# A layer on one core: the expert stage with the second bias added by VectorE, rows gathered six tiles ahead and weights loaded one transfer at a time

## The chip, the core and the metric

The kernel runs on one core of one Trainium2 chip. The metric is the device time of one execution in microseconds (us). Four kinds of engine work side by side and wait for each other through semaphores: TensorE (PE, with its weight loads PEld), VectorE (DVE), ScalarE (ACT) and GpSimd (POOL). SyncE (SP) here only issues transfers and waits. Transfers (DMA) move data between the core's memory (128 partitions) and the device's memory; those issued by GpSimd can gather or scatter rows by a list of indices.

## The reference, cut to what matters

The layer takes 6250 rows of 256 numbers and a graph of 100,000 edges. It normalizes the rows, adds a graph network and an attention with statistics per head, and ends in a mixture of 16 experts. Only this last part is touched:

```python
xn2 = layernorm(x2)                            # 6250 x 256
logits = xn2 @ gate_w + gate_b                 # 16 experts
vals, idx = top_k(logits, 2); w = softmax(vals)
h = relu(xn2 @ w1[e] + b1[e])                  # 512 hidden, e = each chosen expert
expert_out = h @ w2[e] + b2[e]
y = xn2 + sum_k w[k] * expert_out[idx[k]]
out = x2 + layernorm(y) * gamma + beta
```

Since the two weights of a row sum to 1, xn2 can be added once to y, or to each of its two expert rows before they are mixed.

## The kernel before

The rows are held in 49 tiles of 128. Each row goes to two experts, so there are 98 tiles' worth of expert rows; padded per expert they fill at most 114 tiles (XT), which the kernel always works through. Run on these inputs, the reference's router fills 105 tiles: expert 0 has 1, expert 1 has 1, expert 2 has 41, expert 3 has 1, expert 4 has 18, and so on. The last nine tiles are empty; they are computed and land in spare rows.

The kernel is a row of blocks with a barrier between them. The long edge stage (to about 1618 us) sums the graph's messages and makes xn2, which ScalarE stores to the device's memory (`xn2_dram`) and also keeps in `xh` (L1258). The next block, to about 1641 us, makes from the choices a list of row numbers for each tile and each tile's expert. Then comes the **expert stage** (L1844 to L1973), and behind it the **final stage** (L1995 to L2106), which mixes each row's two expert rows and normalizes.

For tile t the expert stage does this:

- GpSimd copies a column of the list to an index tile (`tok_idx`, L1870) and gathers the tile's 128 rows from `xn2_dram` into `tok` (L1884; two buffers).
- TensorE transposes them (L1915), ScalarE copies the transposes out of PSUM (L1949) and copies the tile's expert's first weights to `w1_tile` (L1943), which it finds by a number read from `expert_row`.
- TensorE forms the hidden sums (L1905: eight products, sixteen weight loads in the trace); VectorE adds the first bias and applies relu (four instructions, L1962).
- TensorE reads the expert's number (L1919), puts the second bias into PSUM by a product of a one-hot `pick` (made by VectorE, L1965) with the biases split in bf16 parts (L1923), and adds the second product (L1926: four products, eight weight loads).
- VectorE copies the result to `yrow` (L1971; two buffers), and GpSimd scatters it to the expert rows in device memory (L1876) by `dest_idx` (L1864).

The order on each engine is written out by hand. In pass k TensorE does hidden sums of tile k, transposes of tile k+2 and the second product of tile k-1. GpSimd does the scatter of tile k-1 and behind it the gather of tile k+4. Most passes run in a hardware loop that holds two of them (`run_steps`).

SyncE loads the weights, 512 KB for each half of an expert (L1719, L1720). Expert 0 is loaded ahead of the stage (L1726, L1728). Once the second gather has landed it issues experts 1 to 4, and from then on one expert more whenever one has landed (`WAHEAD` = 4). ScalarE waits for both halves of the tile's expert (`s_wready`).

In the final stage TensorE makes, for each tile of 128 rows, three products: the kept xn2 by the identity (L2023) and the two expert rows by their mixing weights on a diagonal (L2025, L2026). VectorE takes mean and variance from PSUM (L2079, L2084), and scales (L2090, L2098).

## Time and profile before

| | us |
|---|---|
| Median of 3 runs | 2251.18 (2249.81 to 2251.22) |
| The profiled execution's own time | 2252.68 |
| Its span, first to last instruction | 2250.9 |
| Edge stage and all ahead of it, up to about | 1618 |
| Lists of rows, up to about | 1641 |
| Expert stage, first gather to last scatter | 1642.3 to 2163.6 |
| Final stage | 2166.3 to the end |

Busy over the span: PE 1678.2 us (75%), PEld 1414.8, DVE 1377.9, ACT 764.5, POOL 1328.5; the mean granted clock of TensorE is 0.886 of full speed. The share of an engine over the whole span says little here, since the stages have different limits. An "idle before" behind a row gives how long the engine had stood still and what ended it; "issue" there means that the profile shows nothing that it waited for.

### The profile page before, as it was taken

What the parts mean: (1) busy time and instruction counts of PE and PEld (TensorE: products, weight loads), DVE (VectorE), ACT (ScalarE), POOL (GpSimd) and SP (SyncE); (2) the same over time, 40 slices, a digit from 0 to 9 for tenths busy, and PEclk for the clock granted to TensorE, in tenths of its full rate; (3) what the DMA queues carried; (4) which work ended last, traced back from release to release, by engine and by line L of the source; (5) the groups of instructions that cost most, each with busy time, mean ns of one, the idle gap of its engine ahead of it and who ended that gap; (6) DMA issues with size and microseconds to landing.
All of it is one profiled execution on the core that took longest, in us unless ns stands there. A gap on an engine that the chain in (4) does not pass through costs nothing. (4 is left out here: it accounts for less than half of the span.)

```text
span 2250.9 us, 40865 instructions
## 1 busy us (share of the span) xinstructions
PE 1678.2 (75%) x9702; PEld 1414.8 (63%) x9703; DVE 1377.9 (61%) x4034; ACT 764.5 (34%) x2288; POOL 1328.5 (59%) x1455
## 2 busy tenths in 40 slices
PE   6007888237777787888777887776569999999987
PEld 4007877236655666676666665555458888888876
DVE  4999888368776666666666666564433444334348
ACT  5718889100001323323323222221223333333333
POOL 0007888378777777777777777776024555555510
PEclk9558999668878999889999889997789999999999
DMA  5001011354434444444444444448373111111257
GB/s 162 0 0 36 20 36 36 4 164 131 123 105 121 131 127 126 133 127 127 132 127 126 130 122 126 119 126 91 55 262 104 61 62 59 61 61 61 59 201 279
DMA packets 133895, 232.71 MB, mean 103 GB/s; under 512 B 28854, under 2 KB 85784, under 8 KB 133767
## 3 DMA queue, kind: packets, MB, share of 16 engines
q0 software_dynamic: 56096, 144.39, 23.6%
q1 hardware_dynamic: 49975, 60.99, 8.6%
q10 hardware_dynamic: 27696, 25.83, 3.6%
q8 instruction: 55, 0.90, 0.2%
q14 instruction: 73, 0.60, 0.1%
HBM read 188.69 MB, written 42.43 MB: 103 GB/s over the span
## 5 line engine op out<-in xcount | busy, mean ns | idle before, releaser
L1309 POOL DMA_INDIRECT lower<-xn_rows,lower x858 | 851.1, 992 | 270.1 <-issue 234.6
L1334 PE MATMUL bank<-lower 128*128 x960 | 351.0, 451 | 216.4 <-SPq L1183 175.1
L1334 PEld LDWEIGHTS bank<-lower 128*128 128x128 f32 x960 | 172.9, 213 | 300.7 <-issue 290.1
L1472 DVE TENSOR_TENSOR xh<-xh,bank 128x256 f32 x480 | 200.0, 417 | 242.6 <-PE bank L1335 240.9
L1455 DVE TENSOR_SCALAR lower<-iota_n,lower 128x128 f32<-128x128 f32 x960 | 295.4, 361 | 76.0 <-issue 54.5
L606 POOL DMA_INDIRECT edge_records_sorted<-lower x112 | 204.7, 1828 | 209.0 <-ACT lower L755 179.7
L1335 PE MATMUL bank<-lower 128*128 x960 | 322.9, 421 | 0.0
L683 PE MATMUL bank<-lower 128*64 128x128 f32 x1568 | 192.0, 287 | 113.2 <-ACT lower L739 108.8
L683 PEld LDWEIGHTS bank<-lower 128*64 128x64 f32 x1568 | 185.8, 146 | 116.9 <-DVE lower L942 109.4
L1876 POOL DMA_INDIRECT expert_rows<-arena,dest_idx x114 | 114.6, 1005 | 215.4 <-DVE arena L1971 202.9
L1962 DVE TENSOR_SCALAR arena<-bank,b_tile 128x128 f32<-128x128 f32 x456 | 128.3, 344 | 173.5 <-PE bank L1905 173.5
L1335 PEld LDWEIGHTS bank<-lower 128*128 128x128 f32 x960 | 207.2, 216 | 36.8
L1905 PEld LDWEIGHTS bank<-arena 128*128 128x128 f32 x1824 | 224.1, 194 | 9.0 <-issue 3.0
L1926 PE MATMUL bank<-upper,arena 128*128 x912 | 229.0, 395 | 0.0
L1905 PE MATMUL bank<-arena 128*128 128x128 f32 x1824 | 224.6, 277 | 2.6 <-ACT arena L1943 2.6
L1926 PEld LDWEIGHTS bank<-upper,arena 128*128 128x128 f32 x912 | 167.4, 193 | 30.8 <-issue 5.1
L739 ACT ACTIVATE lower<-lower 128x32 f32<-128x32 f32 x784 | 169.3, 309 | 7.4 <-DVE lower L927 6.6
L1250 ACT ACTIVATE std<-mv,eps_col 128x1 f32<-128x1 f32 x49 | 14.4, 295 | 420.8 <-DVE mv L1622 420.8
L1943 ACT ACTIVATE arena<-lower 128x1024 f32 x114 | 120.5, 1057 | 66.6 <-issue 57.8
L1971 DVE COPY arena<-bank 128x256 f32<-128x256 f32 x114 | 48.4, 425 | 150.1 <-PE bank L1926 150.1
L1949 ACT ACTIVATE arena<-bank 128x256 f32<-128x256 f32 x114 | 43.8, 384 | 284.2 <-PE bank L1915 284.2
L1884 POOL DMA_INDIRECT arena<-xn_rows,tok_idx x114 | 109.4, 960 | 40.1 <-issue 32.5
(337 smaller groups left out, 2531.0 us busy)
## 6 DMA issues: line engine op xcount, KB each, us to landing
lower<-xn_rows,lower POOLq DMA_INDIRECT x858
lower<-in_L_ffn_w SPq DMA_DIRECT2D x16, 512.0 KB, 9.0
upper<-in_L_ffn_w SPq DMA_DIRECT2D x16, 512.0 KB, 10.5
xn_rows<-xh SPq DMA_DIRECT2D x7, 896.0 KB, 4.2
lower<-xn_rows ACTq DMA_DIRECT2D x49, 128.0 KB
xn_rows<-lower ACTq DMA_DIRECT2D x49, 128.0 KB
x_plus_beta<-lower ACTq DMA_DIRECT2D x49, 128.0 KB
upper<-in_x SPq DMA_DIRECT2D x1, 6144.0 KB
```

The source lines that it names most:

```text
L606: pool.indirect_dma_start(rec_dram, bass.IndirectOffsetOnAxis(quad_idx[i][:, c:c + 1], 0), quads[i][:, c * QW:(c + 1) * QW], None).then_in ...
L683: mm = pe.matmul(bank[6 + p][0:NQ * QW, 0:P], moving[p][:, e].rearrange("p c w -> p (c w)"), row_hot[p][:, e, :], start=e == 0, stop=e == ...
L739: done = act.activation(moving[p][:, e, :, 1], col_hot[p][:, e, :], ACT.Copy, scale=group_wgt[p][:, e:e + 1])
L1309: pool.indirect_dma_start(edge_rows[:, t % ROUND, :], None, xn_dram, bass.IndirectOffsetOnAxis(source.bitcast(U32)[:, t:t + 1], 0)).then_i ...
L1334: pe.matmul(sums_at(u), edge_sel[:, 2 * u % ESEL, :], rows_flat[:, ds(at, D)], start=True, stop=False)
L1335: pe.matmul(sums_at(u), edge_sel[:, (2 * u + 1) % ESEL, :], rows_flat[:, ds(at + D, D)], start=False, stop=True).then_inc(s_sum, 1)
L1455: dve.tensor_scalar(edge_sel[:, (2 * u + h) % ESEL, :], iota_n[:], lane[:, at:at + 1], weight_s[:, at:at + 1], ALU.is_equal, ALU.mult).the ...
L1472: dve.tensor_tensor(xh[:, at], xh[:, at], sums_at(u), ALU.add).then_inc(s_acc, 1)
L1905: mm = pe.matmul(bank[2 + p][:, m * P:(m + 1) * P], w1_tile[p][:, c * F + m * P:c * F + (m + 1) * P], tokT[p][:, c * P:(c + 1) * P], start ...
L1926: mm = pe.matmul(bank[6 + p][:, 0:D], hidT[p][:, m * P:(m + 1) * P], upper[:, ds(e * (FC * D) + m * D, D)], start=False, stop=m == FC - 1)
L1943: act.activation(w1_tile[p], lower[:, ds(e * (DC * F), DC * F)], ACT.Copy).then_inc(s_w1t, 1)
L1962: dve.tensor_scalar(hidT[p][:, m * P:(m + 1) * P], bank[2 + p][:, m * P:(m + 1) * P], b1_tile[:, ds(t + m * XT, 1)], 0.0, ALU.add, ALU.max ...
```

## The change

- The second bias is no longer a product. All 16 second biases are loaded once, broadcast over the partitions, into `b2_all` (2 MB, in `xh`, whose xn2 is no longer kept: L1258 is gone).
- For each tile VectorE reads the expert's number, adds the gathered rows and the bias row into `yrow` (`biased`, three tiles ahead), and later adds the second product from PSUM to it (`finish`, in place of the copy). The one-hot `pick` is gone.
- The final stage's identity product with xn2 (L2023) is gone, as each expert row now carries its own row.
- `tok` has four buffers and `yrow` six. GpSimd gathers six tiles ahead and reads its indices straight from the lists; the copies of index columns are gone.
- SyncE loads one 512 KB half at a time, and waits for it before it issues the next; it starts when the third gather has landed.
- GpSimd, TensorE and VectorE run all 114 tiles as straight-line code; ScalarE keeps its loop. TensorE reads the next tile's expert number in the middle of the second product.
- Smaller ones: the split of biases in bf16 covers b1 alone, with three loads less.

The core of the diff:

```diff
@@ -353,13 +353,15 @@
+        TOKB, YB = 4, 6
+        carve = carver(xh, NT * D)
+        b2_all = carve(NX * D)
+        yrow = [carve(D) for _ in range(YB)]
-        tok = [carve(D) for _ in range(2)]
+        tok = [carve(D) for _ in range(TOKB)]
-        yrow = [carve(D) for _ in range(2)]
-        pick = [carve(P // 2).bitcast(BF16)[0:96, :] for _ in range(2)]
...
@@ -1255,7 +1252,6 @@
-                    act.activation(xh[:, at], xn2[s % XB], ACT.Copy).then_inc(s_xn2k, 1)
                     act.dma_start(xn2_dram[ds(bucket_now[s] * P, P), :], xn2[s % XB]).then_inc(s_xn2st, 16)
...
-        def load_weights(sp, e):
-            sp.dma_start(w1_sb[:, e], w1[e].rearrange("(c p) f -> p c f", p=P)).then_inc(s_we[e % WAHEAD], 16)
-            sp.dma_start(w2_sb[:, e], w2[e].rearrange("(m p) d -> p m d", p=P)).then_inc(s_we[e % WAHEAD], 16)
 
...
+                sp.dma_start(b2_all, row(b2.rearrange("e d -> (e d)"))).then_inc(s_b2, 16)
...
@@ -1844,90 +1834,92 @@
-                for e in range(NX):
-                    sp.wait_ge(s_we[e % WAHEAD], 32 * (e // WAHEAD + 1))
+                sp.wait_ge(s_we, 32)
+                sp.sem_inc(s_wready, 1)
+                sp.wait_ge(s_tok[2], 16)
+                for e in range(1, NX):
+                    sp.dma_start(w1_sb[:, e], w1[e].rearrange("(c p) f -> p c f", p=P)).then_inc(s_we, 16)
+                    sp.wait_ge(s_we, 32 * e + 16)
+                    sp.dma_start(w2_sb[:, e], w2[e].rearrange("(m p) d -> p m d", p=P)).then_inc(s_we, 16)
+                    sp.wait_ge(s_we, 32 * e + 32)
                     sp.sem_inc(s_wready, 1)
-                    if e == 0:
-                        sp.wait_ge(s_tok[1], 16)
-                        for later in range(1, WAHEAD):
-                            load_weights(sp, later)
-                    if e + WAHEAD < NX:
-                        load_weights(sp, e + WAHEAD)
...
+                def gather(t):
+                    if t >= TOKB:
+                        pool.wait_ge(s_tT, t - TOKB + 1)
+                        pool.wait_ge(s_yb, t - TOKB + 1)
+                    pool.sem_inc(s_apart, 1)
+                    pool.indirect_dma_start(tok[t % TOKB], None, xn2_dram,
+                                            bass.IndirectOffsetOnAxis(rows_idx[:, t:t + 1], 0)).then_inc(s_tok[t % TOKB], 16)
+
+                def scatter(t):
+                    pool.wait_ge(s_yr, t + 1)
+                    pool.sem_inc(s_apart, 1)
+                    pool.indirect_dma_start(y_dram, bass.IndirectOffsetOnAxis(dest_idx[:, t:t + 1], 0),
+                                            yrow[t % YB], None).then_inc(s_yst[t % YB], 16)
+
+                for t in range(-AHEAD, XT):
+                    if t + AHEAD < XT:
+                        gather(t + AHEAD)
+                    if t >= 0:
+                        scatter(t)
+                for b in range(YB):
+                    pool.wait_ge(s_yst[b], 16 * len(range(b, XT, YB)))
...
+                expert = {}
+
+                def load_expert(t):
+                    _, loaded = nc.values_load_multi_w_load_instructions(
+                        expert_row[0:1, t:t + 1], engines=(nc.tensor.engine,), min_val=0, max_val=NX - 1,
+                        skip_runtime_bounds_check_because="a number of an expert")
+                    expert[t] = loaded[0]
+
+                def hidden(t):
+                    p = t % 2
+                    pe.wait_ge(s_tTe, t + 1)
+                    pe.wait_ge(s_w1t, t + 1)
+                    if t >= 2:
+                        pe.wait_ge(s_hr, (t - 1) * FC)
+                    for m in range(FC):
+                        for c in range(DC):
+                            mm = pe.matmul(bank[2 + p][:, m * P:(m + 1) * P],
+                                           w1_tile[p][:, c * F + m * P:c * F + (m + 1) * P],
+                                           tokT[p][:, c * P:(c + 1) * P], start=c == 0, stop=c == DC - 1)
+                    mm.then_inc(s_h, 1)
+
+                def turn(t):
+                    pe.wait_ge(s_tok[t % TOKB], t // TOKB * 16 + 16)
+                    if t >= 2:
+                        pe.wait_ge(s_tTe, t - 1)
+                    for c in range(DC):
+                        mm = pe.transpose(bank[t % 2][:, c * P:(c + 1) * P], tok[t % TOKB][:, c * P:(c + 1) * P], ident[:])
+                    mm.then_inc(s_tT, 1)
+
+                def second(t):
+                    p = t % 2
+                    if t >= 2:
+                        pe.wait_ge(s_yr, t - 1)
+                    pe.wait_ge(s_hr, t * FC + FC)
+                    for m in range(FC):
+                        mm = pe.matmul(bank[6 + p][:, 0:D], hidT[p][:, m * P:(m + 1) * P],
+                                       upper[:, ds(expert[t] * (FC * D) + m * D, D)], start=m == 0, stop=m == FC - 1)
+                        if m == 1 and t + 1 < XT:
+                            load_expert(t + 1)
+                    mm.then_inc(s_y, 1)
+
+                load_expert(0)
+                for t in range(-2, XT + 1):
+                    if 0 <= t < XT:
+                        hidden(t)
+                    if t + 2 < XT:
+                        turn(t + 2)
+                    if t >= 1:
+                        second(t - 1)
...
@@ -1952,25 +1944,37 @@
...
+                LETB = 3
+                def hidden(t):
+                    p = t % 2
+                    dve.wait_ge(s_h, t + 1)
+                    if t >= 2:
+                        dve.wait_ge(s_y, t - 1)
+                    for m in range(FC):
+                        dve.tensor_scalar(hidT[p][:, m * P:(m + 1) * P], bank[2 + p][:, m * P:(m + 1) * P],
+                                          b1_tile[:, t + m * XT:t + m * XT + 1], 0.0, ALU.add, ALU.max).then_inc(s_hr, 1)
+                def biased(t):
+                    e = dve.value_load(expert_row[0:1, t:t + 1], min_val=0, max_val=NX - 1)
+                    dve.wait_ge(s_tok[t % TOKB], t // TOKB * 16 + 16)
+                    if t >= YB:
+                        dve.wait_ge(s_yst[t % YB], t // YB * 16)
+                    dve.tensor_tensor(yrow[t % YB], tok[t % TOKB], b2_all[:, ds(e * D, D)], ALU.add).then_inc(s_yb, 1)
+                def finish(t):
+                    dve.wait_ge(s_y, t + 1)
+                    dve.wait_ge(s_yb, t + 1)
+                    dve.tensor_tensor(yrow[t % YB], yrow[t % YB], bank[6 + t % 2][:, 0:D], ALU.add).then_inc(s_yr, 1)
+                dve.wait_ge(s_b2, 16)
+                for t in range(-LETB, XT + 1):
+                    if 0 <= t < XT:
+                        hidden(t)
+                    if t + LETB < XT:
+                        biased(t + LETB)
+                    if t >= 1:
+                        finish(t - 1)
...
@@ -2020,9 +2024,8 @@
-                        pe.matmul(mixed, ident[:], xh[:, t * D:(t + 1) * D], start=True, stop=False)
-                        pe.matmul(mixed, diag[t % NDG * TOPK], first_row(t), start=False, stop=False)
+                        pe.matmul(mixed, diag[t % NDG * TOPK], first_row(t), start=True, stop=False)
```

```order
L1905 MATMUL bank<-arena 128x128 x7
L1915 MATMUL bank<-ident,arena 128x128 [waits rows_transpose_copied,rows_landed1]
L1915 MATMUL bank<-ident,arena 128x128
L1919 REGISTER_ALU
L1919 TENSOR_LOAD expert_row
L1919 ISA x2
L1923 MATMUL bank<-bias_split,arena 128x256 [waits expert_rows,bias_pick]
L1924 REGISTER_ALU
L1926 ISA [waits expert_hidden]
L1926 MATMUL bank<-upper,arena 128x256
```

The same place now:

```order
L1889 MATMUL bank<-arena 128x128 x7
L1899 MATMUL bank<-ident,arena 128x128 [waits rows_transpose_copied,rows_landed0]
L1899 MATMUL bank<-ident,arena 128x128
L1908 ISA [waits expert_hidden,expert_rows]
L1908 MATMUL bank<-upper,arena 128x256
L1908 ISA
L1908 MATMUL bank<-upper,arena 128x256
L1876 TENSOR_LOAD expert_row
L1908 ISA
L1908 MATMUL bank<-upper,arena 128x256
```

The reading of the number has moved from between the transposes and the bias product to between the second and the third of the four products, and is for the tile after; the bias product is gone.

GpSimd in the loop before (the second half of it):

```order
L1864 COPY dest_idx<-arena 128x1
L1870 ISA [waits rows_landed1]
L1870 COPY tok_idx<-rows_all 128x1
L1873 REGISTER_ALU
L1874 REGISTER_ALU [waits result_index_staged0]
L1876 DMA expert_rows<-arena,dest_idx 27137x256 [waits expert_rows]
L1884 DMA arena<-xn_rows,tok_idx 128x256 [waits row_index_staged1,rows_transposed]
```

GpSimd now, at the start of the stage:

```order
L1854 DMA arena<-xn_rows,rows_idx 128x256 x4
L1854 DMA arena<-xn_rows,rows_idx 128x256 [waits rows_transposed,rows_with_bias] x3
L1860 DMA expert_rows<-xh,dest_idx 27137x256 [waits expert_rows]
L1854 DMA arena<-xn_rows,rows_idx 128x256 [waits rows_transposed,rows_with_bias]
L1860 DMA expert_rows<-xh,dest_idx 27137x256 [waits expert_rows]
```

Seven gathers now stand ahead of the first scatter, the first four of them without a wait, and behind scatter t comes gather t+7.

SyncE's weight transfers before:

```order
L1719 DMA lower<-in_L_ffn_w 128x2x512 [waits weights_of_expert0,rows_landed1]
L1720 DMA upper<-in_L_ffn_w 128x4x256
L1719 DMA lower<-in_L_ffn_w 128x2x512
L1720 DMA upper<-in_L_ffn_w 128x4x256
L1719 DMA lower<-in_L_ffn_w 128x2x512
L1720 DMA upper<-in_L_ffn_w 128x4x256
L1719 DMA lower<-in_L_ffn_w 128x2x512
```

And now:

```order
L1841 DMA lower<-in_L_ffn_w 128x2x512 [waits expert_weights_loaded,rows_landed2]
L1843 DMA upper<-in_L_ffn_w 128x4x256 [waits expert_weights_loaded]
L1841 DMA lower<-in_L_ffn_w 128x2x512 [waits expert_weights_loaded]
L1843 DMA upper<-in_L_ffn_w 128x4x256 [waits expert_weights_loaded]
L1841 DMA lower<-in_L_ffn_w 128x2x512 [waits expert_weights_loaded]
```

Each transfer now waits for the one before it.

## Rows read from the trace of the kernel before

**Rows 1.** Busy time by stretch; columns: stretch, length, engines (instructions), PEclk, DMA share, GB/s.
```profile
1648.00:1700.00 52.00, 39.13 (x210) 34.03 (x210) 12.82 (x46) 12.66 (x18) 16.44 (x30) 0.83 0.99 341
1700.00:2100.00 400.00, 380.82 (x2506) 338.00 (x2505) 161.19 (x558) 133.25 (x186) 210.67 (x370) 1.00 0.19 61
2175.00:2235.00 60.00, 59.62 (x265) 49.33 (x264) 52.79 (x178) 30.91 (x96) 0.00 (x0) 1.00 0.97 360
```

**Rows 2.** Timeline of weight loads, two passes: start, length, engine, line, operation, count, [idle before].
```profile
1802.11 1.97 PEld L1905 LDWEIGHTS bank<-arena 128*128 128x128 f32 x16
...
1804.21 0.10 PEld L1923 LDWEIGHTS bank<-bias_split,arena 96*128 96x128 bf16 x1
1804.32 1.60 PEld L1926 LDWEIGHTS bank<-upper,arena 128*128 128x128 f32 x8
1805.95 1.97 PEld L1905 LDWEIGHTS bank<-arena 128*128 128x128 f32 x16
1807.87 0.21 PEld L1915 LDWEIGHTS bank<-ident,arena 128*128 128x128 f32 x2
1808.71 0.10 PEld L1923 LDWEIGHTS bank<-bias_split,arena 96*128 96x128 bf16 x1 [0.62 <-issue]
...
1810.57 1.97 PEld L1905 LDWEIGHTS bank<-arena 128*128 128x128 f32 x16
```

**Rows 3.** Timeline of VectorE and GpSimd in the same passes.
```profile
1802.61 0.42 DVE L1971 COPY arena<-bank 128x256 f32<-128x256 f32 x1 [1.54 <-PE bank L1926]
...
1803.86 1.01 POOL L1876 DMA_INDIRECT expert_rows<-arena,dest_idx  x1 [2.08 <-DVE arena L1971]
...
1804.50 1.13 DVE L1962 TENSOR_SCALAR arena<-bank,b_tile 128x128 f32<-128x128 f32 x4 [1.46 <-PE bank L1905]
...
1805.18 0.96 POOL L1884 DMA_INDIRECT arena<-xn_rows,tok_idx  x1 [0.31 <-issue]
```

**Rows 4.** Line L1884, stretch 1705 to 2100: its gathers' time to landing.
```profile
DMA to landing us min/median/max: 2.7/2.7/3.6
```

**Rows 5.** Line L1884, stretch 1648 to 1700: the same.
```profile
DMA to landing us min/median/max: 5.4/5.8/6.2
```

**Rows 6.** Timeline of the expert stage's first tiles, and its last.
```profile
1642.26 0.97 POOL L1884 DMA_INDIRECT arena<-xn_rows,tok_idx  x1 [0.82 <-POOL tok_idx L1870]
...
1648.00 3.54 PEld L1905 LDWEIGHTS bank<-arena 128*128 128x128 f32 x16
...
1660.25 1.97 PEld L1905 LDWEIGHTS bank<-arena 128*128 128x128 f32 x16
...
2155.42 1.97 PEld L1905 LDWEIGHTS bank<-arena 128*128 128x128 f32 x16
```

**Rows 7.** DMA issues by line, 1618 to 1640: size, median us to landing.
```profile
lower<-in_L_ffn_w SPq DMA_DIRECT2D x1, 512.0 KB, 4.4
upper<-in_L_ffn_w SPq DMA_DIRECT2D x1, 512.0 KB, 3.8
```

**Rows 8.** DMA issues over the whole span: size, median us to landing.
```profile
upper<-in_L_ffn_w SPq DMA_DIRECT2D x16, 512.0 KB, 10.5
```

**Rows 9.** Line L1615, VectorE's sequencer reading a number: ns min/median/max, first and last start.
```profile
L1615 DVEq TENSOR_LOAD <-bucket_of_i x49: 304/315/325, 707.1 to 1603.0; - x49
...
L1615 DVEq SEQ_ASSERT  x49: 23/23/41, 707.7 to 1603.6; - x49
```

**Rows 10.** Timeline 1562.5 to 1564.5, GpSimd and VectorE.
```profile
1562.76 0.95 POOL L1309 DMA_INDIRECT lower<-xn_rows,lower  x1 [0.31 <-issue]
1562.90 0.42 DVE L1627 TENSOR_TENSOR lower<-lower 128x256 f32<-128x256 f32 x1
```

**Rows 11.** Waits over the span: engine, line, releaser, us in total, times, longest us.
```profile
POOL lower L1309 <- issue: 234.6, 769, 0.6
```

**Rows 12.** Timeline of GpSimd behind its loop's end.
```profile
2152.28 1.00 POOL L1876 DMA_INDIRECT expert_rows<-arena,dest_idx  x1 [5.61 <-issue]
```

**Rows 13.** Timeline of weight loads in the final stage.
```profile
2174.34 0.50 PEld L2023 LDWEIGHTS bank<-xh,ident 128*128 128x128 f32 x2 [0.46 <-DMA upper<-expert_rows]
...
2216.97 0.30 PEld L2023 LDWEIGHTS bank<-xh,ident 128*128 128x128 f32 x2 [0.44 <-DVE upper L2090]
```

More of the change, by code:

```diff
@@ L399, in gps_layer @@
         tile_expert = sb("tile_expert", [P, 1])
-        rows_all = sb("rows_all", [P, XT])
+        rows_idx = sb("rows_idx", [P, XT], U32)
+        dest_idx = sb("dest_idx", [P, XT], U32)
         bucket_of_i = sb("bucket_of_i", [P, NT], I32)[:, 0:NT]
         b1_tile = sb("b1_tile", [P, FC * XT])
-        tok_idx = [sb(f"tok_idx{i}", [P, 1], U32) for i in range(2)]
-        dest_idx = [sb(f"dest_idx{i}", [P, 1], U32) for i in range(2)]
         pick_all = sb("pick_all", [96, P], BF16)
-        ones_b = sb("ones_b", [96, P], BF16)
         expert_row = sb("expert_row", [1, P], I32)
@@ L786, in _ @@
                 dve.memset(eps_col[:], LN_EPS).then_inc(s_dve, 1)
-                dve.memset(ones_b[:], 1.0).then_inc(s_dve, 1)
                 dve.memset(blockdiag, 0.0).then_inc(s_dve, 1)
-                dve.wait_ge(s_dve, n.add(3))
+                dve.wait_ge(s_dve, n.add(2))
                 for q in range(P // HD):
@@ L1699, in _ @@
                         unit(u)
-        s_we = [sem(f"weights_of_expert{e}") for e in range(WAHEAD)]
+        s_we = sem("expert_weights_loaded")
         s_gap = sem("gate_gaps")
@@ L1808, in _ @@
                 dve.wait_ge(s_dve, n.add(2))
[L1809 removed]
+                dve.scalar_tensor_tensor(rows_idx[:], tile_i3, float(P), listed, ALU.mult, ALU.add).then_inc(s_rows, 1)
                 dve.wait_ge(s_rows, 2)
[L1811 removed]
+                dve.scalar_tensor_tensor(dest_all, rows_idx[:], float(TOPK), plane_i, ALU.mult, ALU.add).then_inc(s_dve, 1)
                 dve.wait_ge(s_dve, n.add())
[L1813 removed]
+                dve.tensor_tensor(dest_idx[:], dest_all, spare_at, ALU.max).then_inc(s_rows, 1)
                 dve.wait_ge(s_b1, 1)
@@ L1817, in _ @@
                 dve.wait_ge(s_rows, 3)
-        s_tki = [sem(f"row_index_staged{i}") for i in range(2)]
-        s_tok = [sem(f"rows_landed{i}") for i in range(2)]
+        s_tok = [sem(f"rows_landed{i}") for i in range(TOKB)]
         s_tT = sem("rows_transposed")
@@ L1832, in gps_layer @@
         s_y = sem("expert_sums")
+        s_yb = sem("rows_with_bias")
         s_yr = sem("expert_rows")
-        s_ydi = [sem(f"result_index_staged{i}") for i in range(2)]
-        s_yst = [sem(f"expert_rows_scattered{i}") for i in range(2)]
+        s_yst = [sem(f"expert_rows_scattered{i}") for i in range(YB)]
         assert XT % 2 == 0
         E_STEPS = (-2, XT, 2, (XT - 2) // 2)
-        AHEAD = 4
-        G_STEPS = (-AHEAD, XT, 2, (XT - AHEAD) // 2)
+        AHEAD = 6
         def is_tile(t):
@@ L1887, in _ @@
-                run_steps(pool, step, *G_STEPS)
-                for p in range(2):
-                    pool.wait_ge(s_yst[p], 16 * (XT // 2))
+                def gather(t):
[5 more added lines that the diff above has]
+                                            bass.IndirectOffsetOnAxis(rows_idx[:, t:t + 1], 0)).then_inc(s_tok[t % TOKB], 16)
@@ L1954, in _ @@
             def _(dve):
-                def step(j, k):
-                    t, p, _ = tile_at(j, k)
-                    if is_tile(t):
-                        dve.wait_ge(s_h, t + 1)
-                        if over(t - 1):
-                            dve.wait_ge(s_y, t - 1)
-                        for m in range(FC):
-                            dve.tensor_scalar(hidT[p][:, m * P:(m + 1) * P], bank[2 + p][:, m * P:(m + 1) * P],
-                                              b1_tile[:, ds(t + m * XT, 1)], 0.0, ALU.add, ALU.max).then_inc(s_hr, 1)
-                        dve.tensor_scalar(pick[p], ones_b[:], pick_all[:, ds(t, 1)], None, ALU.mult).then_inc(s_pk, 1)
-                    t, p, half = tile_at(j, k - 1)
-                    if is_tile(t):
-                        dve.wait_ge(s_y, t + 1)
-                        if over(half):
-                            dve.wait_ge(s_yst[p], half * 16)
-                        dve.tensor_copy(yrow[p], bank[6 + p][:, 0:D]).then_inc(s_yr, 1)
```

86 lines of the change are left out of this document (9 added, 77 removed).

## The prediction

> **What bounds the kernel now.** I read the busy time by stretch first. In the expert stage from 1700 to 2100 us TensorE is busy for 381 of 400 us at a full clock, VectorE for 161, GpSimd for 211, and the DMA engines for 19% [rows 1]. So this stage is nearly TensorE's; what is to be had is the rest of its idle time and whatever work leaves it. From 1648 to 1700 it is another picture: TensorE busy 39 of 52 us, clock 0.83, DMA share 0.99. In the final stage (2175 to 2235) everything is full: TensorE 59.6 of 60 us, VectorE 52.8, DMA 0.97.
>
> Next the timeline of weight loads, since they show TensorE's pace without the modelled ends. Two passes differ: one takes 1805.95 - 1802.11 = 3.84 us, the next 1810.57 - 1805.95 = 4.62 us, of which 0.62 us is idle ahead of the bias product [rows 2]. The timeline of the other engines tells why. VectorE's copy ends at 1803.03, the scatter starts 0.83 us later, the gather 1.32 us behind it at 1805.18 [rows 3], and it lands 2.7 us later [rows 4], at 1807.88, which is where the transposes of the long pass stand (1807.87). TensorE's sequencer is held at that wait, reads the expert's number only then, and the array runs dry. So a loop copy, scatter, gather, landing, transposes, about one pass long, costs every second pass 0.78 us.
>
> Last the first tiles and the last: hidden sums of tile 2 start at 1660.25, those of tile 113 at 2155.42 [rows 6]. That is 495.2 us for 111 passes, 4.46 each, against 4.23 for the mean of the two passes above. Much of the rest is in the stretch to 1700, where gathers land after 5.4 to 6.2 us beside the weights [rows 5].
>
> **The change part by part.** Sums are made against the profiled execution, 2252.68 us (span 2250.9 and 1.8 around it); the median of the runs is 1.5 lower.
>
> *TensorE per pass.* The bias product takes 1804.32 - 1804.21 = 0.11 us of the short pass [rows 2]. Without it the short pass is 3.73 us; I take 3.75 for every pass, as nothing shows below that. Reading the number now stands behind two of the four products. What hides it is the work handed over before: with no gather to hold the sequencer these are at least the four weight loads of those two products, 0.8 us (eight take 1.60). In the short pass the same reading is hidden already. I cost it at nothing; uncovered it would be up to the 0.62 us of the long pass. Bounds of a pass: 3.73 and 4.35.
>
> *The gather's loop.* VectorE's finish of tile t falls in the start of pass t+2; the gather behind it lands 0.83 + 1.32 + 2.7 = 4.85 us later and is for tile t+7, whose rows VectorE wants in pass t+4 behind the hidden sums: two passes and 2 us later, 9.5 us. So 4.6 us of slack, and 1.1 us even with a landing of 6.2 us. GpSimd's own pass is scatter and gather, 1.32 us each with the gap behind, plus 0.83 us of waking: 3.5 us of 3.75. The new waits stand ahead of gathers, with only scatters behind, for buffers used three passes ago.
>
> *VectorE per pass.* Four relu instructions 1.13 us [rows 3]; reading the number 0.6 us plus the 0.02 of its check [rows 9]; the bias add 0.42, as the 128x256 addition of two tiles in memory [rows 10]; the addition from PSUM about the copy's 0.42 [rows 3]. Together 2.6 us of 3.75. If the number's reading hides behind the relus it is 2.0. Behind its new waits stand the finish and the next relus, for which TensorE waits only two passes later.
>
> Against this speaks a rule of the Trainium skill, page SBUF — State Buffer, on the two sides of the memory: an addition with two operands in SBUF and a GpSimd instruction that reads SBUF lock each other out for a whole instruction. By it the bias add could wait for a gather's 0.96 us, and VectorE's pass would be 3.6 us, still under 3.75. The trace disagrees: the addition of 1562.90 starts 0.14 us into a gather of 0.95 us and ends after its usual 0.42 us [rows 10].
>
> So passes 2 to 112 give 111 x 3.75 = 416.3 us in place of 495.2: **-78.9 us**.
>
> *The start.* The first gather no longer waits for its index tile, and starts about 1641.3 instead of 1642.26; the third, two steps of 1.27 us on (gather and gap), at 1643.8 and lands at 1646.6. Then come four transfers in a row for experts 1 and 2. One alone lands after 4.4 and 3.8 us [rows 7], in the old stream after 10.5 in the median [rows 8]. Four alone are 16.4 us, and SyncE's turns 0.4: expert 2 is ready at 1663.4, its copy takes 1.06 us, and the hidden sums of tile 2 start at 1664.6, 4.3 us late, since tiles 0, 1 and 2 have three different experts. TensorE meanwhile stands still twice for some 5 us, so these sums may run at the slow level, as those of tile 0 did (3.54 us in place of 1.97 [rows 6]): 1.6 us. From there expert 2 lasts 41 tiles, and all others load within some 27 x 4.1 = 110 us. Sum **+5.9 us**; bounds +2 (warm, landings beside little traffic) and +26 (every landing as in the old stream: 4 x (10.5 - 4.1) = 25.6 on top, less what overlaps).
>
> The page DMA: Bandwidth & Descriptors of the Trainium skill (Anatomy of one DMA) has 2.0 us and the bytes at 436 GB/s for one transfer, an estimate of 3.2 us for 512 KB. By it the four would take 12.8 us and the start would cost 2.3; the trace's 4.4 and 3.8 decide.
>
> *Loading the biases.* 2 MB ahead of expert 0's first half. At the 360 GB/s of [rows 1] 5.8 us, beginning about 1619, while the lists are being made and nobody needs either before 1641: nothing; without that cover 5.8. ScalarE's dropped copy (49, off the path in a stage that GpSimd's gathers pace), the shorter split and the one-hots: nothing, bound 1 us.
>
> *The end of the stage.* Two bias products less behind the last hidden sums: **-0.2 us**.
>
> *The final stage.* 265 product records in 60 us at six a tile are 44 tiles, 1.36 us each; without L2023 TensorE would need a third less. VectorE has 52.8 us of work in these 60, and DMA is at 0.97. So the gain ends where VectorE is full: 7.2 us in this stretch if nothing else held, 0 if DMA does. At the start TensorE waits for rows anyway (0.46 us), and in the middle for VectorE to free a bank (0.44 us) [rows 13], which shows that they are already near a tie. I take **-4.5 us**, bounds 0 and -9.
>
> Sum: -78.9 + 5.9 - 0.2 - 4.5 = -77.7; 2252.7 - 77.7 = 2175.0, and as a median 1.5 less: **2173 us**.
>
> **The rivals.**
>
> *The number's reading shows.* If TensorE's queue runs dry in each pass, as in the long pass, by 0.3 to 0.62 us: 114 x 0.45 = 51 us, 2225. For it: the reading cost 0.62 in every second pass. Against: there the sequencer had just been held by the gather, and in the short passes nothing shows.
>
> *VectorE becomes the bound.* Its pass must reach more than 3.75 us: 2.6, the 0.96 of a gather that locks it, and 0.6 of waits between the steps make 4.2, which gives 111 x 0.45 = 50 us more, 2223. Rows 10 speak against it.
>
> *Weights one at a time starve the start.* With landings of 10.5 us expert 2 is ready 25.6 us later: 2199. Against: DMA share was 0.99 then and would be about 0.5 now.
>
> *Slower: straight-line code isn't fetched in time.* Behind its loop's end GpSimd stood still for 5.61 us with nothing to wait for [rows 12]. If TensorE met such a stop in its long straight code once in five tiles, 23 x 5.6 = 129 us would give 2302; it ends the gain from 14 stops on, one in eight tiles. Against it: 858 gathers of the edge stage stand in straight code too, and the longest such wait among them is 0.6 us [rows 11]. The page Runtime: NRT & Kernel Launch of the Trainium skill (Instruction fetch mechanics) says the same: fetching runs ahead in straight code and stalls at a taken branch; by that rule the stops would go with the loops.
>
> **How the numbers follow.** My forecast 0.73; the reading 0.12; VectorE 0.04; the starved start 0.06; the fetch 0.05. The forecast's own range is 2164 (final stage -9, start +2) to 2185 (a pass of 3.85). To hold 8 in 10 the range is cut below at 2162 and reaches to the middle of the reading's case, 2212. Faster than before by over 0.2% (4.5 us; about what a measurement can tell from no change) are all cases but the last: 0.94; the same 0.01; slower 0.05.
>
> **What would show it.** Right: weight loads of the hidden sums 3.75 us apart with no idle ahead of any from tile 2 on; no wait of TensorE for a landing of rows; first of tile 2 near 1664.6; weight transfers landing after about 4 us each; end of the stage near 2089; final stage shorter by about 4 us with VectorE over 95% busy. Wrong: idle time ahead of the third product of each tile (the reading), relus late against their sums (VectorE), or gaps of some 5 us in TensorE with nothing that ends them (the fetch).

## The result and the profile after

| | before | after |
|---|---|---|
| Median of the runs | 2250.49 us (2248.23 to 2251.22, 4 runs) | 2169.99 us (2169.39 to 2170.17, 4 runs) |
| Span of the profiled execution | 2250.9 | 2168.3 |
| Hidden sums of tile 2 start | 1660.25 | 1664.42 |
| Hidden sums of tile 113 start | 2155.42 | 2078.31 |
| 111 passes between them | 495.2 | 413.9 |
| From there to the end of the span | 95.5 | 90.0 |

The ratio is 0.9643, 95% interval 0.9627 to 0.966. The forecast was 2173 us.

The busy time by stretch, as in [rows 1] (stretch, length, PE, PEld, DVE, ACT, POOL with their instructions, PEclk, DMA share, GB/s):

```profile
1648.00:1700.00 52.00, 45.14 (x296) 42.42 (x296) 20.74 (x66) 17.04 (x25) 20.69 (x22) 0.92 0.59 188
1700.00:2050.00 350.00, 350.00 (x2439) 330.60 (x2438) 176.65 (x564) 135.51 (x188) 183.56 (x188) 1.00 0.31 97
```

The second row is the result in short: TensorE is busy for 350.00 of 350 us, where it had been for 381 of 400. The first row shows that the weights no longer fill the queues (DMA share 0.59 instead of 0.99), and that 7 us of TensorE are still lost there.

The timeline of a pass, weight loads, VectorE and GpSimd, as in [rows 2] and [rows 3]:

```profile
1801.62 0.97 POOL L1854 DMA_INDIRECT arena<-xn_rows,rows_idx  x1 [0.30 <-issue]
...
1801.89 0.41 DVE L1963 TENSOR_TENSOR xh<-arena,xh 128x256 f32<-128x256 f32 x1
1802.38 1.97 PEld L1889 LDWEIGHTS bank<-arena 128*128 128x128 f32 x16
...
1802.80 0.42 DVE L1968 TENSOR_TENSOR xh<-xh,bank 128x256 f32<-128x256 f32 x1 [0.49 <-PE bank L1908]
1804.06 0.98 POOL L1860 DMA_INDIRECT expert_rows<-xh,dest_idx  x1 [1.48 <-DVE xh L1968]
1804.27 0.25 PEld L1899 LDWEIGHTS bank<-ident,arena 128*128 128x128 f32 x2
...
1804.49 1.60 PEld L1908 LDWEIGHTS bank<-upper,arena 128*128 128x128 f32 x8
1804.58 1.13 DVE L1955 TENSOR_SCALAR arena<-bank,b_tile 128x128 f32<-128x128 f32 x4 [1.36 <-PE bank L1889]
...
1805.35 0.96 POOL L1854 DMA_INDIRECT arena<-xn_rows,rows_idx  x1 [0.30 <-issue]
...
1806.11 1.97 PEld L1889 LDWEIGHTS bank<-arena 128*128 128x128 f32 x16
```

1806.11 - 1802.38 = 3.73 us, and no weight load has an idle time ahead of it. Every pass from tile 3 on looks so. All waiting has moved to VectorE (1.36 us for TensorE's sums) and GpSimd (1.48 us for VectorE's finish). The bias add of 1801.89 runs inside a gather of GpSimd and takes its 0.41 us.

The numbers are read by the sequencers (ns min/median/max; VectorE's, then TensorE's):

```profile
L1959 DVEq TENSOR_LOAD <-expert_row x94: 298/304/316, 1700.1 to 2047.2; - x94
...
L1959 DVEq FUSED_REGOPS  x94: 190/190/190, 1700.5 to 2047.5; - x94
```
```profile
L1876 PEldq TENSOR_LOAD <-expert_row x94: 296/300/542, 1702.3 to 2049.4; - x94
```

TensorE's reading of 0.30 us is there in each of the 94 passes and costs none of them a gap.

The start, as in [rows 6] and [rows 7], with SyncE's issues (SPq) and ScalarE's copies of first weights (L1935):

```profile
1640.84 0.62 DVE L1808 COPY b_tile<-bank 128x456 f32<-128x456 f32 x1
1642.70 0.95 POOL L1854 DMA_INDIRECT arena<-xn_rows,rows_idx  x1 [23.15 <-POOLq L1714]
...
1647.97 0.37 SPq L1841 DMA_DIRECT2D lower<-in_L_ffn_w  x1
...
1651.63 0.37 SPq L1843 DMA_DIRECT2D upper<-in_L_ffn_w  x1
...
1655.55 0.37 SPq L1841 DMA_DIRECT2D lower<-in_L_ffn_w  x1
1655.61 1.06 ACT L1935 ACTIVATE arena<-lower 128x1024 f32 x1 [7.14 <-SPq L1845]
...
1656.78 3.30 PEld L1889 LDWEIGHTS bank<-arena 128*128 128x128 f32 x16 [4.66 <-issue]
1659.30 0.37 SPq L1843 DMA_DIRECT2D upper<-in_L_ffn_w  x1
...
1663.30 1.06 ACT L1935 ACTIVATE arena<-lower 128x1024 f32 x1 [6.36 <-SPq L1845]
...
1664.42 1.86 PEld L1889 LDWEIGHTS bank<-arena 128*128 128x128 f32 x16 [2.60 <-issue]
```

SyncE's issues stand 3.66, 3.92 and 3.75 us apart, since each waits for the half before. ScalarE waits 7.14 us for expert 1 and 6.36 for expert 2, and TensorE stands still meanwhile.

The final stage:

```profile
2110.00:2155.00 45.00, 34.23 (x143) 25.20 (x141) 44.62 (x152) 23.70 (x72) 0.00 (x0) 1.00 1.03 391
```

VectorE is busy for 44.62 of 45 us; it was 52.8 of 60 [rows 1]. TensorE has room now.

### The profile page after: what moved, and what is told of

It reads as the page before. It is cut to its first block and busy times, and to the rows that moved or that the text cites. A ratio compares the mean times of both kernels' runs of the same rounds, so it can differ in the third digit from the quotient of the medians.

```text
span 2168.3 us, 38376 instructions
## 1 busy us (share of the span) xinstructions
PE 1607.2 (74%) x9490; PEld 1379.1 (64%) x9490; DVE 1391.0 (64%) x4033; ACT 749.5 (35%) x2239; POOL 1291.6 (60%) x1227
## 3 DMA queue, kind: packets, MB, share of 16 engines
q8 instruction: 79, 1.29, 0.3%
## 5 line engine op out<-in xcount | busy, mean ns | idle before, releaser
L1860 POOL DMA_INDIRECT expert_rows<-xh,dest_idx x114 | 112.2, 984 | 183.0 <-DVE xh L1968 168.6
L1908 PE MATMUL bank<-upper,arena 128*128 x912 | 215.6, 379 | 0.0
L1854 POOL DMA_INDIRECT arena<-xn_rows,rows_idx x114 | 110.7, 971 | 60.7 <-issue 33.5
L1935 ACT ACTIVATE arena<-lower 128x1024 f32 x114 | 120.5, 1057 | 72.2 <-issue 57.8
L1372 PE MATMUL bank<-lower,upper 128*128 128x128 f32 x784 | 109.8, 299 | 0.0
```

The source lines that it names most:

```text
L1908: mm = pe.matmul(bank[6 + p][:, 0:D], hidT[p][:, m * P:(m + 1) * P], upper[:, ds(expert[t] * (FC * D) + m * D, D)], start=m == 0, stop=m = ...
L1935: act.activation(w1_tile[p], lower[:, ds(e * (DC * F), DC * F)], ACT.Copy).then_inc(s_w1t, 1)
```

## The experiments

The first four kernels ran on a chip on which the kernel before took 2504 us, because its edge stage was longer there; so of these the times inside the expert stage and the gain over the kernel before beside them are used; a ratio to 2504 us looks smaller than the same gain does against 2250, and is not to be set beside 0.9643. Their block of lists begins at 1856 us and later, where the changed kernel on the first chip has it at 1619. "111 passes" is always from tile 2's hidden sums to tile 113's in the trace; it was 413.9 us after the change on the first chip.

### Gathers less far ahead, and the number read earlier

Theory A: the gain comes from both, and each alone is worth little. Rival: one of them carries it.

```diff
-        TOKB, YB = 4, 6
+        TOKB, YB = 2, 6
...
-        AHEAD = 6
+        AHEAD = 4
...
-                sp.wait_ge(s_tok[2], 16)
+                sp.wait_ge(s_tok[1], 16)
...
-                LETB = 3
+                LETB = 2
```

> The changed kernel with the gathers as short ahead as before: two row buffers in place of four, gathers four tiles ahead, the bias add two tiles ahead. Theory A (the gather's loop cost time only because the reading of the expert's number stood behind its wait): the rows land 0.84 + 4.85 = 5.7 us after a pass begins, and the transposes want them at 3.73 + 1.9 = 5.6, so a pass grows from 3.73 to 3.8 or 3.9 us and the time from 2170 to 2178 - 2190. Theory B (the long lookahead itself is the gain): passes go back to about 4.2 us, time near 2225.

Measured: ratio 0.9769 (0.9709 to 0.9828, 2 runs), 56.6 us less than the kernel before on this chip; 111 passes 451.9 us, 4.07 each. That is neither theory's number, and nearer to B's.

The number read ahead of the second product of its own tile, with six tiles ahead:

```diff
                 def second(t):
+                    load_expert(t)
...
-                        if m == 1 and t + 1 < XT:
-                            load_expert(t + 1)
```

> The changed kernel with TensorE's reading of the expert's number put back ahead of the second product, gathers still six tiles ahead. Theory A: with no gather to hold the sequencer the reading hides behind the hidden sums and transposes, passes stay 3.73 us, time 2168 - 2173. Rival (the place of the reading is the gain): up to 0.6 us per pass shows, 3.73 to 4.3, time near 2235.

Measured: 0.9652 (0.9601 to 0.9702, 2 runs), 85.8 us less; 111 passes 414.9 us, nearly all 3.73 each. Theory A.

Both edits:

> Both at once: gathers short ahead (two row buffers, four tiles ahead) and the number read ahead of the second product. Theory A (the two together made the long passes): long and short passes take turns again with about 0.6 us idle ahead of the second product, mean pass 4.1 to 4.2, time 2210 - 2225. Rival (each by itself costs what it costs, and nothing together): the sum of what the other two runs show over 2170.

Measured: 0.9882 (0.981 to 0.9953, 2 runs), 28.2 us less; 111 passes 469.1 us, 4.23 each.

So where the reading stands is worth 1 us at most with deep gathers, and 469.1 - 451.9 = 17 us with short ones; going back to the short depth alone costs 38 us. I had expected 8 to 20 for it. To see whether the other chip was the cause, the two kernels with short gathers ran again beside a kernel before of 2254.54 us.

> The changed kernel with two gather buffers, gathers four tiles ahead and the bias add two tiles ahead, the same edit as the first short gather, but beside a kernel before that takes about 2251 us. Theory B (the loop finish, scatter, gather, landing has no slack in every pass, whatever the edge stage does): again about 38 us over the 111 passes, so 2208 us, ratio about 0.981. Theory A (the 38 us came from late landings on that other chip; here a landing of 2.7 us leaves most passes at 3.73): 2178 to 2190 us, ratio 0.968 to 0.973.

Measured: 2210.73 us (2202.51 to 2214.39, 4 runs), 0.9799 (0.9773 to 0.9826); 111 passes 455.2.

> The same with TensorE reading the expert's number behind the transposes, as the kernel before does. Theory B: 55 us over the 111 passes, 2225 us, ratio about 0.989. Theory A (reading shows only in every second pass, 0.62 us each, 34 us beside the short gather's 8 to 20): 2210 to 2225 us. What then is left to the kernel before (about 26 us at 2225) should be the bias products (12), the identity product (5) and what loops and copies of indices cost (the rest, about 9).

Measured: 2225.22 us (2219.9 to 2232.31, 4 runs), 0.9882 (0.9851 to 0.9913); 111 passes 470.2.

Theory B's 2208 was met, and Theory A's range missed: the chip was not the cause. (2225 was both theories' number for the second kernel, which decides nothing between them.) The timeline of the short gather (weight loads, VectorE's finish, GpSimd) shows what is:

```profile
1908.76 0.20 PEld L1899 LDWEIGHTS bank<-ident,arena 128*128 128x128 f32 x2 [0.47 <-DMA arena<-xn_rows,rows_idx]
1908.96 1.59 PEld L1908 LDWEIGHTS bank<-upper,arena 128*128 128x128 f32 x8
...
1910.99 0.42 DVE L1968 TENSOR_TENSOR xh<-xh,bank 128x256 f32<-128x256 f32 x1 [1.02 <-PE bank L1908]
1912.26 0.98 POOL L1860 DMA_INDIRECT expert_rows<-xh,dest_idx  x1 [2.01 <-DVE xh L1968]
...
1913.55 0.96 POOL L1854 DMA_INDIRECT arena<-xn_rows,rows_idx  x1 [0.30 <-issue]
...
1916.66 0.20 PEld L1899 LDWEIGHTS bank<-ident,arena 128*128 128x128 f32 x2 [0.38 <-DMA arena<-xn_rows,rows_idx]
```

From transposes over second product, finish, scatter, gather and landing to the transposes that wait for it are 1916.66 - 1908.76 = 7.90 us, and this chain has two passes, 7.46 us. Here 3.11 us of it are from the gather's start to the transposes; with the 2.7 us of an undisturbed landing [rows 4] it would be 7.49, and the shortest two passes in this trace, from 1883.19 to 1890.68, take just that. So the loop has nothing to spare even then, and a landing that is slower is paid in full. From 1700 to 2120 the transposes waited for rows before 35 tiles of 102, 29.6 us in sum (who waited for these gathers: us, times):

```profile
  PEld bank L1899: 29.6, 35
```

The mean pass is 455.2 / 111 = 4.10. I had taken every landing at 2.7 us, and with it the rows to be nearly in time. What ties the loop is the order of GpSimd's instructions, more than the buffers: each of these 102 gathers stood still for 0.30 us and waited for nothing, so its buffer was already free and it only had its turn behind the scatter. Whether two buffers with the gather put one scatter earlier would do as well was not run.

The kernel before has the same loop:

```profile
1799.41 0.20 PEld L1915 LDWEIGHTS bank<-ident,arena 128*128 128x128 f32 x2
```

From these transposes to those at 1807.87 [rows 2] are 8.46 us, two passes, with a reading of the number (0.62 us idle) and a bias product in the chain.

With the early reading the second product is late as well. The idle time ahead of its weight loads (last column) over the stage, first with the short gather alone, then with both edits:

```profile
L1908 PEld LDWEIGHTS bank<-upper,arena 128*128 128x128 f32 x822 | 148.3, 191 | 17.3 <-issue 0.3
```
```profile
L1909 PEld LDWEIGHTS bank<-upper,arena 128*128 128x128 f32 x813 | 149.5, 194 | 38.5 <-issue 21.1
```

21.2 us more, in which no weights were loaded while the number was read: 0.36 us most times. Some of it is given back, since the transposes now wait 19.1 us for rows in place of 29.6; 15 us remain between 470.2 and 455.2.

How deep must it be? Three buffers, five tiles ahead:

```diff
-        TOKB, YB = 4, 6
+        TOKB, YB = 3, 6
...
-        AHEAD = 6
+        AHEAD = 5
```

> The changed kernel with three gather buffers and gathers five tiles ahead, the bias add still three ahead. By the slack counted in the prediction (4.6 us with six ahead) one pass less leaves 0.9 us with a landing of 2.7 us and none where a landing takes over 3.6: nearly all passes stay at 3.73, a few near the weights at the start are late, 2170 to 2178 us. The rival: the slack was counted too large, since VectorE's bias add, now waited for by the very next gather, closes a loop of its own: 2185 to 2200 us.

Measured: 2169.74 us (2165.49 to 2174.53, 4 runs), 0.9623 (0.9603 to 0.9644), beside the same kernel before; 111 passes 413.9. Its busy time by stretch, with TensorE busy throughout as after the change:

```profile
1700.00:2050.00 350.00, 350.00 (x2440) 330.74 (x2439) 177.39 (x564) 135.41 (x188) 182.85 (x188) 1.00 0.32 98
```

One more pass gives the chain of 7.90 us 11.19 to run in, and nothing is late any more. The fourth buffer and the sixth tile are reserve. (Buffers and depth were changed together in all these runs, and so was the bias add's distance, two tiles ahead with two buffers and three otherwise.)

### The bias product

```diff
                 def second(t):
+                    pe.matmul(bank[6 + p][:, 0:D], pick_all[:], bias_split[:, 0:D], start=True, stop=False)
```

> The changed kernel with a bf16 product of the old bias product's shape (96x128 by 96x256) put ahead of each second product, from constant tiles; it adds wrong numbers to the rows, and only its price is meant. Theory: TensorE is bound with nothing idle, so each of 114 costs the 0.11 us of its slot in the short pass, 12.5 us, time 2182 - 2184. Rival (it would hide beside the rest): 2170. Rival (a change between number formats costs more, 0.24 us as in the long pass): 2197.

Measured: 0.9708 (0.9653 to 0.9764, 2 runs), 71.6 us less than the kernel before on this chip; 111 passes 426.2 us, so 12.3 more than 413.9, 0.11 a pass. Its own loads in the trace:

```profile
L1906 PEld LDWEIGHTS bank<-bias_split,pick_all 96*128 96x128 bf16 x91 | 8.9, 98 | 0.0
```

### The order of the weights

The changed kernel with the old order of weights (experts 1 to 4 at once, one more for each that has landed):

> The changed kernel with the weights as before: experts 1 to 4 issued together once the third gather has landed, then one more as each lands. Theory A (six tiles ahead hides the late gathers, so one at a time only delays the start): hidden sums of tile 2 start near 1661 in place of 1664.4, no stall to 1700, time 2166 - 2169. Theory B (one at a time is what keeps gathers from landing late): gathers land after 5 to 6 us, TensorE waits again beside the weights, time 2172 - 2182.

Measured: 2166.6 us (2164.63 to 2167.3, 4 runs), 0.9618 (0.9602 to 0.9634). 111 passes take 414.0.

The start of tile 2 as such can't be compared between traces, since the edge stage ahead does not end at the same time in each. The block of lists, from its first instruction to the first gather, takes 23.8 us in every trace of the kernel before and 23.4 in every one of the changed kernel, so times are best counted from the first gather:

| | lists begin | first gather | tile 2 | tile 2 behind the first gather |
|---|---|---|---|---|
| before | 1618.51 | 1642.26 | 1660.25 | 17.99 |
| before, one transfer at a time | 1617.03 | 1640.78 | 1662.30 | 21.52 |
| after | 1619.31 | 1642.70 | 1664.42 | 21.72 |
| after, old order of weights | 1619.11 | 1642.51 | 1661.12 | 18.61 |
| after, three experts ahead of the stage | 1618.55 | 1641.95 | 1655.58 | 13.63 |
| after, short gather | 1621.94 | 1645.33 | 1666.91 | 21.58 |
| after, short gather and early reading | 1616.37 | 1639.78 | 1661.17 | 21.39 |

So the old order starts tile 2 3.1 us earlier than one transfer at a time. In the stretch from 1648 to 1700 the gathers of this kernel land late again:

```profile
DMA to landing us min/median/max: 5.1/6.1/6.5
```

as in [rows 5], but now no pass from tile 2 on is longer than 3.74. The reverse, the kernel before with one transfer at a time:

> The kernel before with the weights one transfer at a time, nothing else. Theory: hidden sums of tile 2 start some 4 us later, but the waits for rows in the stretch to 1700 (three of about 3 us, each with a slow clock behind) go: tile 9 starts some 10 us earlier, time 2239 - 2244. Rival (the late start is given back nowhere): 2254.

Measured: 2253.25 us (2246.66 to 2256.32, 8 runs), 1.0001 (0.9989 to 1.0014). The rival's number. In its trace tile 2 is 3.5 us later behind the first gather and the 111 passes take 487.6 us, 7.6 less; the waits beside the weights did shrink, and tile 9 is 7.8 us earlier. But the span of that one execution is only 5.3 us shorter, 1.5 of it because the edge stage ended earlier, and the eight timed runs show no gain. The kernel before also varies in this stretch: with its final stage alone changed (below) the 111 passes took 497.8. One transfer at a time helps only a gather that is on the path, and costs its own delay at the start.

### The identity product in the final stage

```diff
-                        pe.matmul(mixed, ident[:], xh[:, t * D:(t + 1) * D], start=True, stop=False)
```

> The kernel before without the final stage's identity product, so xn2 is left out of y. It measures what that product's leaving is worth by itself. Theory: as in the changed kernel, VectorE becomes full and the time behind the last hidden sums falls by 5 to 5.5 us: 2245. Rival (the transfers hold it and the gain in the changed kernel came from elsewhere): under 2 us.

Measured: 2246.96 us (2244.64 to 2250.94, 8 runs), 0.9979 (0.9969 to 0.999), 4.8 us less than the 2251.77 of the kernel before beside it. From tile 113 to the end: 89.9 us instead of 95.5. Its final stage is that of the changed kernel:

```profile
2190.00:2235.00 45.00, 34.29 (x144) 25.69 (x143) 44.30 (x150) 23.71 (x72) 0.00 (x0) 1.00 1.03 391
```

### Three experts loaded ahead of the stage

What is left in the start are the waits for experts 1 and 2. So in the changed kernel experts 1 to 3 are loaded like expert 0 while the lists are made, each second half as soon as the lists' memory is free, and the rest one at a time from expert 4:

```diff
-                sp.dma_start(w1_sb[:, 0], ...).then_inc(s_we, 16)
-                sp.wait_ge(s_lists, TOPK * FC)
-                sp.dma_start(w2_sb[:, 0], ...).then_inc(s_we, 16)
+                for e in range(WAHEAD):
+                    sp.dma_start(w1_sb[:, e], ...).then_inc(s_we, 16)
+                for e in range(WAHEAD):
+                    sp.wait_ge(s_lists, TOPK * FC * (e + 1))
+                    sp.dma_start(w2_sb[:, e], ...).then_inc(s_we, 16)
...
-                for e in range(1, NX):
+                for e in range(WAHEAD, NX):
```

> The changed kernel with experts 1 to 3 loaded already in the block of lists, each second half as soon as the lists no longer need its place; from expert 4 on one transfer at a time. Theory: tiles 1 and 2 no longer wait for weights, the hidden sums of tile 2 start near 1657 in place of 1664.4, time 2161 - 2164. Rival (these transfers slow the block of lists or its stores): as much is lost there, 2168 - 2172.

Measured: 2161.42 us (2157.89 to 2163.21, 4 runs), 0.9596 (0.958 to 0.9612): the fastest of all. That is 8.6 us under the changed kernel's 2169.99, measured beside a kernel before of 2251.77 where that one had 2250.49. Its timeline of weight loads:

```profile
1651.26 2.55 PEld L1891 LDWEIGHTS bank<-arena 128*128 128x128 f32 x16
...
1655.58 1.97 PEld L1891 LDWEIGHTS bank<-arena 128*128 128x128 f32 x16
```

Behind the first gather tile 2 starts 8.1 us earlier than after and 4.4 earlier than before (table above), and 111 passes take 414.0. The block of lists takes its 23.4 us as without these transfers, so the rival's loss there does not exist.

## Why the prediction was right

The time was 2170.0 for a forecast of 2173, and between the profiled spans -82.6 us for a sum of -77.7. (The medians differ by 80.5; the profiled execution before was 1.5 above its median, as the prediction allowed for.) Term by term:

- **The passes: -78.9 forecast, -81.3 measured.** The pass of 3.75 was taken two hundredths above the short pass without its bias product; it is 3.73 everywhere, and 111 x 0.02 is the difference. The causes named hold: the bias product is 0.11 a pass (12.3 us), and most of the rest is the gather's loop with the reading behind it. One reading of the rows was wrong: the prediction calls this loop "about one pass long", which is its part from the copy's end to the landing (4.85 us). The whole loop is two passes long and paces both, 8.46 us in the pair of [rows 2]; the change was large enough to end it either way, but the estimate for two buffers went wrong by it. Undoing the depth and the place of the reading brings back 470.2 - 413.9 = 56 us. From there to the 495.2 of before are 25: 12.3 of the bias product, up to 7.6 of the weights (one trace, which the timed runs don't confirm), and the rest, some 5 or more, not taken apart (loops, index copies; VectorE's bias add stays in).
- **The reading of the number at nothing.** Right, but for a reason that reaches further than the prediction's: even at its old place it costs nothing when no gather holds the sequencer. Its new place is a second cover for the same gap.
- **The gather's loop.** The slack of 4.6 us was never used up, also not at landings of 6.1 us. The count was good: in the median VectorE's bias add starts 7.74 us behind its gather's start, 5.0 more than a landing of 2.7, and with three buffers 4.01, 1.3 more, where the count leaves 0.9. My later estimate that two buffers would cost 8 to 20 us failed: it took every landing at 2.7 us, where the loop has no slack and each slower landing adds to it.
- **GpSimd's pass** was put at 3.5 of 3.75 us of work and waking; its two steps start 1.29 us apart and it waits 1.48 us for the finish, of which 0.84 us is behind the finish's end (1803.22 to 1804.06). So 1.29 + 0.96 + 0.84 = 3.1 us, as the prediction counted the gap behind the gather too. When GpSimd is late and nothing has to wake it, its passes take 2.56 us (scatters at 2056.57, 2059.12 and 2061.68).
- **VectorE's pass** was put at 2.6 us: relus 1.13, reading 0.30 + 0.19 + 0.02 for its check, adds 0.41 and 0.42, together 2.47.
- **The lock between VectorE and GpSimd.** By the rule of the Trainium skill (SBUF — State Buffer, SBUF: two separate sides), as the prediction applied it, the bias add would wait for the gather beside it. It starts 0.27 us into a gather and takes 0.41; over the 94 passes of 1700 to 2050 the line's idle time is 0.1 us in sum. So this pair of instructions doesn't lock. The same page (Who interferes with whom) itself says that its own trial saw a `tensor_tensor` not stall transfers issued by GpSimd; the trace agrees with that, and the prediction had left it out. The bias add's row (count, busy us, mean ns, idle before):

```profile
L1963 DVE TENSOR_TENSOR xh<-arena,xh 128x256 f32<-128x256 f32 x94 | 38.9, 414 | 0.1
```

- **The start: +5.9 forecast, +4.2 measured, and partly by luck.** Of the 4.2, 0.8 is not the change's: the edge stage ended that much later in this execution (between 1616.4 and 1623.1 in traces of kernels that share it). The first gather comes 0.4 us sooner behind the begin of the lists (forecast 0.96), as it starts 1.24 us behind VectorE's last copy of the block (1641.46) where it was 1.59. The rest, 3.7, lies behind the first gather, 3.1 of it from the order of the weights. Tile 2 was forecast at 1664.6 and came at 1664.42 because errors cancelled: the transfers began 1.4 us later than forecast (1647.97, not 1646.6), and the four took 15.3 us to ScalarE's copy (1663.30), not 16.8. The 1.6 us of a slow clock for tile 2's sums did not come: their weight loads took 1.86 us at a granted clock of 1.00, while tile 1's, behind an idle time of 4.66 us, took 3.30 at 0.54.
- **The estimate by the Trainium skill's DMA: Bandwidth & Descriptors** (Anatomy of one DMA), 3.2 us for 512 KB alone, is below the 3.66 to 3.92 measured between issues; by it tile 2 would have come some 2 us earlier. The page fits its figure to transfers issued by GpSimd, and these are issued by SyncE.
- **End of the stage and final stage: -4.7 forecast, -5.5 measured.** The identity product alone brings 5.6 in the trace and 4.8 in the medians. The limit named is the one that came: VectorE at 99% of the stage.
- **Straight code.** No gap of TensorE in 350 us, so none of the stops feared. But the row that this rival was made from [rows 12] was read wrongly, and its stop did not go with the loop. Of the 5.61 us GpSimd could not use 2.1, since the copy that it waits for ended only at 2148.79; the scatter came 3.49 us behind it, and the kernel before has the same stop in the middle of its loop. The changed kernel, which has no loop on GpSimd, has it twice: the finishes ahead of them end at 1862.92 and 2053.24, and the scatters come 3.33 us behind them.

```profile
1909.14 1.00 POOL L1876 DMA_INDIRECT expert_rows<-arena,dest_idx  x1 [4.44 <-issue]
```
```profile
1866.25 0.98 POOL L1860 DMA_INDIRECT expert_rows<-xh,dest_idx  x1 [3.96 <-DVE xh L1963]
...
2056.57 0.98 POOL L1860 DMA_INDIRECT expert_rows<-xh,dest_idx  x1 [3.97 <-DVE xh L1963]
```

By the Trainium skill's rule (Runtime: NRT & Kernel Launch, Instruction fetch mechanics), as the prediction used it, these stops would have gone. They stayed in code that has no branch, so a taken branch is not their cause.
- **The range.** Its upper end, 2212, is called the middle of the reading's case, but 0.3 to 0.62 us over 114 tiles is 2207 to 2244, with the middle at 2225. The result does not hang on it.

What the prediction did not see is that one part of the change is not worth its price: one transfer at a time. The prediction priced its later start and named no gain for it. It is needed for nothing once the gathers are far ahead, and costs 3 us.

## What to carry to other kernels

Add up the whole chain from a tile's transposes to the next ones that wait on it, through every engine and through the order of instructions on each, and compare it with the passes that it has; here 7.5 us at best and 7.90 in the rows shown, against 7.46, cost 10% of a stage. One tile more of depth (with its buffer) ended every wait for rows, and with two more even landings of 6 us were free. Work that an engine's sequencer does between two products shows only when something else has held that sequencer; take the holder away before moving the work. A measure that protects a late transfer (one at a time) should be tried again when the transfer is no longer late, and loads for the first tiles belong ahead of the stage.

## What was not expected of the hardware

- The same kernel took 2504 us on one chip and 2250 to 2255 in the medians of the other comparisons. Of this one difference the traces show that the edge stage ended 230 to 260 us later; why is open. The expert stage was the same on both (451.9 and 455.2 us for the short gather's 111 passes).
- At two places of the stage GpSimd starts an instruction late, the same in all thirteen traces: scatter 53 or 54 and, 51 tiles on, scatter 104 or 105 in the changed kernels, 54 and 109 in the kernel before. The scatter follows its finish (or copy) by 3.3 to 3.5 us where 0.84 is usual; with three buffers the first of the two stops falls on the gather ahead. With gathers six tiles ahead TensorE does not notice; in the kernel before the stop made one pass 6.99 us long, with the short gather 6.23 and 7.57. The tiles are the same on the chip with the longer edge stage, so the places hang on the position in the instructions and not on time. The cause is open.
- The edge stage, the same in all changed kernels, ended at times up to 6.8 us apart in their traces (begin of the lists from 1616.37 to 1623.13). What lies behind it repeats far better: the block of lists to 0.02 us, tile 2 behind the first gather with one transfer at a time to about 0.5 us (21.39 to 21.91), the 111 passes of the deep kernels to 0.2 us (413.9, 414.0, 414.0, 413.9). The 111 passes of the kernels with short gathers vary by some 3 us (451.9 and 455.2).
